# Attention: GpSimd makes the next pair sum before it issues a triple's second fold

## What is computed

```python
q, k, v = ...                                  # 16 heads of 32 channels, from h @ Wqkv.T + bqkv
energy = jnp.einsum('bhqd,bhkd->bhqk', q, k)
att = jax.nn.softmax(energy, axis=-1) / D ** 0.5
out = jnp.einsum('bhqk,bhkd->bhqd', att, v)    # then a projection, the residual and a norm
```

## Time and profile before

| | us |
|---|---|
| median of 3 runs | 2997.95 (2995.87 to 3001.31) |
| the profiled execution | 2999.27 |
| its span, from first to last instruction | 2997.5 |
| TensorE busy | 2882.8 (96%) |
| GpSimd busy | 1802.6 (60%) |
| VectorE, ScalarE busy | 2013.3, 1512.2 |
| granted clock of TensorE, mean | 0.984 |
| attention stage, from about | 1290 to 2890 |

### The profile page before, as it was taken

How to read it: one execution, slowest core, us unless ns; L and a number is a source line. 1 busy time by engine, 2 the same in 40 slices (tenths; PEclk the granted TensorE clock), 3 DMA queues, 4 the chain that set the end, 5 groups by cost and what they waited for, 6 DMA issues and landing times.

```text
span 2997.5 us, 41315 instructions
## 1 busy us (share of the span) xinstructions
PE 2882.8 (96%) x15018; PEld 1915.0 (64%) x15018; DVE 2013.3 (67%) x3559; ACT 1512.2 (50%) x2756; POOL 1802.6 (60%) x797
## 2 busy tenths in 40 slices
PE   4899999999999998999999999999999999999997
PEld 2787788888888886755555555555555555555456
DVE  6873332222233556678888888888888887888549
ACT  3552233232333222156666666666666666666654
POOL 2775310111110442158898899888899888989864
PEclk7999999999999999999999999999999999999999
DMA  6543100000001657486668866687766778666668
GB/s 213 174 142 127 43 29 0 29 29 28 29 29 43 212 206 226 171 192 127 138 138 181 185 137 141 129 192 157 165 134 132 165 166 172 138 136 129 148 194 290
DMA packets 155051, 405.64 MB, mean 135 GB/s; under 512 B 12102, under 2 KB 30506, under 8 KB 134343
## 3 DMA queue, kind: packets, MB, share of 16 engines
q0 software_dynamic: 22608, 164.64, 27.5%
q1 hardware_dynamic: 132248, 238.41, 26.0%
HBM read 144.51 MB, written 92.31 MB: 79 GB/s over the span
## 4 chain that ended last, share of the span: by engine, by line
POOL 21%; DMA 13%; PE 12%; issue 8%; DVE 2%; ACT 0%; POOLq 0%; SPq 0%; DVEq 0%; ACTq 0%
POOL pair L1947 19%; DMA pair<-pair 12%; PE psum L1724 3%; PE psum L1712 3%; PE psum L1697 3%; POOL v_out L1913 1%; DVE part_max L1833 1%; PE psum L1752 1%; POOL pair L1930 1%; DMA p_att_lo<-att_parts 1%; PE psum L37 1%; PE psum L39 1%; PE psum L38 1%; ACT probs L1803 0%; DVE p_h L2137 0%
## 5 line engine op out<-in xcount | busy, mean ns | idle before, releaser
L1833 DVE TENSOR_REDUCE part_max<-psum 128x1 f32<-128x512 f32 x1984 | 1213.6, 682 | 171.6 <-PE psum L1697 166.2
L1803 ACT ACTIVATE probs<-psum 128x512 f32<-128x512 f32 x2048 | 1046.1, 612 | 495.8 <-PE psum L1712 490.4
L1947 POOL TENSOR_TENSOR pair<-probs 128x2048 f32<-128x2048 f32 x255 | 1197.8, 4777 | 97.0 <-ACT probs L1803 78.9
L1712 PE MATMUL psum<-queries,keys 128*128 128x512 f32 x2048 | 839.3, 412 | 11.1 <-ACT probs L1803 5.4
L1697 PE MATMUL psum<-keys,queries 128*128 128x512 f32 x1984 | 796.1, 402 | 0.8
L1712 PEld LDWEIGHTS psum<-queries,keys 128*128 128x128 f32 x2048 | 383.7, 188 | 343.6 <-issue 215.0
L1724 PE MATMUL psum<-probs,values 128*32 128x512 f32 x4096 | 511.8, 600 | 0.0
L1697 PEld LDWEIGHTS psum<-keys,queries 128*128 128x128 f32 x1984 | 374.0, 189 | 92.1 <-DVE part_max L1833 43.1
L1077 DVE TENSOR_TENSOR h_lo<-w_stage,h_hi 128x512 fp32r<-128x512 f32 x128 | 100.7, 787 | 486.1 <-ACT h_hi L986 486.0
L979 ACT ACTIVATE w_stage<-psum,b_col 128x512 f32<-128x512 f32 x128 | 88.3, 690 | 483.2 <-PE psum L39 482.4
L1724 PEld LDWEIGHTS psum<-probs,values 128*32 128x32 f32 x4096 | 107.0, 109 | 242.1 <-ACT probs L1803 133.7
(11 more groups left out here) (337 smaller groups left out, 3708.7 us busy)
## 6 DMA issues: line engine op xcount, KB each, us to landing
pair<-pair POOLq DMA_DIRECT2D x157, 1024.0 KB, 7.4
queries<-q_parts SPq DMA_DIRECT2D x96, 256.0 KB, 6.3
keys<-k_parts SPq DMA_DIRECT2D x42, 512.0 KB, 10.7
s_x<-in_x_dram SPq DMA_DIRECT2D x8, 1024.0 KB, 7.8
s_y<-in_x_dram SPq DMA_DIRECT2D x8, 1024.0 KB, 5.5
y_rows<-s_y SPq DMA_DIRECT2D x8, 1024.0 KB, 4.7
q_parts<-qk_hi SPq DMA_DIRECT2D x32, 256.0 KB, 2.0
q_parts<-qk_lo SPq DMA_DIRECT2D x32, 256.0 KB, 2.3
```

Of the source, the lines that this page charges most:

```text
L1712: nc.tensor.matmul(psum[:, SC + unit % 3, :], keys[place(count)[0]][:, h, kt * P:(kt + 1) * P], queries[count % NQ][:, h, :], start=True, ...
L1803: act.activation(probs[tile % NPROB][:, h, :], psum[:, SC + unit % 3, :], ACT.Exp).then_inc(exp_ready, 1)
L1833: dve.tensor_reduce(part_max[:, h * TT + qt, kc:kc + 1], max_slot(), AX.X, ALU.max).then_inc(max_read, 1)
L1947: pool.tensor_tensor(pair[number % NPAIR][:, :, :], probs[2 * number % NPROB][:, :, :], probs[(2 * number + 1) % NPROB][:, :, :], ALU.add) ...
```

## The change

In the loop over the pair sums of `gpsimd` in `attention_stage`, a fold whose predecessor is a fold as well (the second of a triple: numbers 2 and 5 of a block) is no longer issued behind its own pair sum, but behind the next one (3 and 6). Its waits are those of before. First folds of triples (1 and 4), fold 7 and the folds of the last block stay where they were.

```diff
--- before.py
+++ after.py
@@ -1946,8 +1946,10 @@
                 fold_wait(pool, FOLDS[old + 1])
             pool.tensor_tensor(pair[number % NPAIR][:, :, :], probs[2 * number % NPROB][:, :, :],
                                probs[(2 * number + 1) % NPROB][:, :, :], ALU.add).then_inc(pair_ready, 1)
-            if number in FOLDS:
+            if number in FOLDS and number - 1 not in FOLDS:
                 fold(number)
+            if number - 1 in FOLDS and number - 2 in FOLDS:
+                fold(number - 1)
         normalise(BLOCKS - 1)
         split_result(BLOCKS - 1)
```

## The result

The changed kernel takes 3032.33 us (median of 4 runs, 3028.89 to 3035.18) against 2998.48 us before (4 runs, 2995.87 to 3001.31): **slower**, the ratio is 1.0114, with a 95% interval from 1.0102 to 1.0127. Its profiled execution took 3032.92 us with a span of 3031.1 us.

What follows compares the result with a forecast made beforehand. TensorE was taken to bound the stage with almost no slack. Terms +14 (queries), +59 (keys), −5 (returned waits) and −3 (tail) sum to +65 us on 2999.3, giving 3064; forecast 3040 to 3090, stated range 3000 to 3110.

Steps and rivals of the forecast that it cites:

- (b): Rival: only the six key-loading blocks stall, 5 us each, clock stays up, query tie won; +27 us, 3008 to 3040; chance 0.17.
- Removed: GpSimd at sum 6: today's 2.23 us idle behind fold 4 goes; GpSimd gains 1.6 us there.
- (1): GpSimd's sum 5 and the next block's sum 0 each wait up to 1 us for a fold; little net change.
- (2): Fold 5 is issued 5.1 us later, at 1494.0; its slack before TensorE's addition shrinks from 8 us to 2.6; costs nothing alone.
- (4): Six blocks where SP loads keys: fold 5 behind them stalls TensorE 6.5 us plus 3.3 of lower clock; +59 us, bounds 30 to 86.
- (3): Ordinary blocks: fold 5 falls behind SP's query load, 0.8 us wait in 17 of 23 blocks; +14 us, bounds 0 to 35.
- The trap: Sum 0, held by fold 5, delays the next fold 5 past the query load's start, so the lateness repeats in ordinary blocks.
- (5): Returned: half of the old fold waits and lower clock, −5 us (0 to −10), and −3 us at the tail.
- The tail: Block 30: sum 6 begins some 5 us sooner, returning ScalarE's waiting; −3 us, bounds 0 and −4.
- (a): Rival: DMA engines take turns between queues; fold 5 lands after 9.3 us, some 1 us stall; some 3000 us; chance 0.14.
- (c): Rival, faster: GpSimd reaches sum 6 over 1 us sooner, fold 5 is issued ahead of the loads; 2986 us; chance 0.08.
- (d): Rival: GpSimd becomes the bound, held by folds at each block's start and midst, never catching up; 3090 to 3130; chance 0.13.

## Why the prediction was right

It was right in direction and, for the largest term, in mechanism; in size it was too high: +65 us forecast, +34 measured. 3032 us lie below its own forecast of 3040 to 3090, inside the stated range only because that range took in rival (b), whose +27 is the nearer figure. By its steps:

- *Removed and (1), GpSimd.* Right in kind: the wait ahead of folds is gone, two waits per block take its place. Of the two, the one ahead of sum 5 is up to 1 us in most ordinary blocks, as I had said; the one ahead of sum 0 is 2.1 to 3.9 us and not up to 1, since fold 5 takes 8.9 to 10.7 us beside the queries.
- *(2), the slack of fold 5.* Right: replayed at 1494.0 in block 3, issued at 1494.01.
- *(4), the keys.* The stall is right nearly to the digit: issue replayed at 1593.6, found at 1593.59; landing 13.6, found 14.1; idle 5.0, found 5.09. The two terms of the price were too large. The six stalls are 5.5 us on average, not 6.5: fold 5 stayed at most 1.9 us behind the keys. And I had charged half of a fall's whole length behind the stall, where its first part lies within it: of the 37.5 us at the lower level TensorE was busy for 28, half of which is 14. From one block's end to the next, by SP's first issue there, the six take 56.1 to 57.3 us where an ordinary one takes 49.2 (1592.86 to 1648.96, for one), together +47 and not +59: 32.7 of idle and some 14 for the clock; filling the stalls gave back 8, net of 3.4 that the filling cost.
- *(3), the queries.* This step failed in its size: +14 forecast, and there are five waits of 0.4 to 0.5 us in ordinary blocks. The trap did not close. I let GpSimd carry sum 0's delay on through the block; in the rows it has caught up at sum 6, which starts behind its exponentials in nearly every ordinary block (0.87 us of wait in block 3), so that fold 5 is issued 0.5 us ahead of the queries again and again. I had taken 4.7 us for a sum in (1); the 255 take 4.6 on average now, and 4.8 before.
- *(5), what comes back.* This failed too: I kept half of the old waits, as bound by the load. Fold 2, issued when the keys are through, took 9.3 us in block 5 where it took 13.6, and what is left of its waits is one of 0.7 us, so that nearly all of the 10 us came back. The tail returned 2.6 us by the last block's length, near the 3 forecast; a fall of the clock of 3.4 us near 2843 us of before is gone there as well, and which of the two returned the time was not tested.
- *The sum.* By the spans: 47.1 for the six blocks, 2.3 for the queries, 0.7 left of fold 2's waits, less 10.5 of old waits and lower clock, less 2.6 at the tail, make 37.0. The stage behind attention is 2.3 us shorter than in the profile of before and the stages ahead of it 1.2, which leaves 33.5; the two spans differ by 33.6. These last two I take for spread between executions; no run was made for them.
- *The rivals.* (a), turns, put fold 5's landing at 9.3 us and its stall at 1; they were 14.1 and 5.09. It has a part in the truth all the same: my rule that a fold stands behind what SP has queued covers the 6.0 us to its first packet, and turns cover the 8.0 after it. (b) had the time nearly right, the stalls at 5 us and the query tie won; its one fault is the clock, which did fall. (c) wanted fold 5 ahead of the loads: in ordinary blocks it is, by 0.5 us, which is no more than a tie, and what came back is fold 2's, whose new place lies behind most of the keys (9.3 us in block 5). (d), GpSimd as the bound, fell: it catches up within each block. The statement of the Trainium skill in "DMA: Bandwidth & Descriptors", "Queues, rings and completion order", that an engine changes between the rings it has work for packet by packet, fits the trace from 1599.6 us on (188 packets against 197) and not the 6.0 us before, in which the fold was outstanding and had none.

## What to carry to other kernels

A transfer that is issued later, to spare its engine a wait, is moved along the other queues too: look up what SP issues at the old and the new moment before pricing the wait. Slack that covers a transfer alone (2.6 us here) does not cover it behind 1.5 MB that were issued 0.7 us sooner, and to be first it has to be issued some half a microsecond ahead. And a change that moves two things alike may be worth splitting: half of this one gains 0.5%.

## What the runs showed that I had not expected

A fold's landing depends on half a microsecond: with the queries first, 10.5 to 10.7 us when it is issued 0.5 us or more ahead of the keys, 12.3 to 13.8 when it is 0.0 to 0.2 ahead. The kernel with the later addition has the same step: 11.0 us at 0.7 ahead, in block 15, and 13.3 to 14.6 at 0.2 or more behind. The lower clock costs half of the time that TensorE works at it, 14 of 28 us, and nothing for the part that lies within the stall. And TensorE's additions and GpSimd's buffers were tied so closely that an appointment moved by two tiles changed where the loss stood and not how large it was.
